# A graph-network block loop on one core: first relus put ahead of the gathered rows' work, next block's transposes put between the halves of the second layer

## The reference, cut to what matters

```python
h0 = layernorm(x)                                   # 6250 nodes x 256
out1 = segment_sum(edge_attr, dst)                  # 100000 edges x 96, dst is sorted
out2 = where(cnt > 0, segment_max(edge_attr, dst), 0)
out3 = out1 / max(cnt, 1)
h = concat([h0, out1, out2, out3, u[0]], axis=1)
h = relu(h @ W1 + b1) @ W2 + b2                     # hidden 1024, out 256
x = x + (h + h0)
x = x + ffn(layernorm(x))                           # router, top 2 of 16 experts, layer norm
```

## Time and profile before

| | us |
|---|---|
| median of 3 runs | 1315.99 (1310.38 to 1318.45) |
| the profiled execution's own time | 1307.6 |
| its span in the profile | 1305.9 |
| TensorE busy in the span | 1129.7 (87%) |
| ScalarE busy | 647.9 (50%) |
| GpSimd busy | 830.1 (64%) |
| VectorE busy | 788.1 (60%) |
| mean granted TensorE clock | 0.925 of full speed |

### The profile page before, as it was taken

How to read it: one execution, slowest core, us unless ns; L and a number is a source line. 1 busy time by engine, 2 the same in 40 slices (tenths; PEclk the granted TensorE clock), 3 DMA queues, 4 the chain that set the end, 5 groups by cost and what they waited for, 6 DMA issues and landing times.

```text
span 1305.9 us, 27758 instructions
## 1 busy us (share of the span) xinstructions
PE 1129.7 (87%) x6584; PEld 973.4 (75%) x6585; DVE 788.1 (60%) x3031; ACT 647.9 (50%) x1972; POOL 830.1 (64%) x1112
## 2 busy tenths in 40 slices
PE   2007999999999999999999999999999999999354
PEld 1006888877888878888888888899999999998011
DVE  5989899799799989953444114642222222221697
ACT  5954566566656655665565342223332323333464
POOL 5767666775676566666665145656665666664786
PEclk7557999999999999999999999999999999999665
DMA  9976678768777677486111258756665666663665
GB/s 313 294 267 219 225 283 299 255 209 307 273 277 271 251 234 269 165 285 203 49 37 38 81 194 308 261 186 202 212 213 196 214 213 206 211 212 123 207 224 171
DMA packets 131052, 282.65 MB, mean 216 GB/s; under 512 B 25742, under 2 KB 38293, under 8 KB 130831
## 3 DMA queue, kind: packets, MB, share of 16 engines
q1 hardware_dynamic: 93947, 218.28, 49.4%
q0 software_dynamic: 26048, 43.47, 10.5%
q10 hardware_dynamic: 10964, 19.96, 4.4%
HBM read 167.15 MB, written 114.25 MB: 215 GB/s over the span
## 4 chain that ended last, share of the span: by engine, by line
PE 54%; DMA 11%; issue 11%; POOL 10%; ACT 7%; DVE 4%; POOLq 2%; ACTq 0%; SPq 0%; DVEq 0%
PE ps L1222 14%; PE ps L1230 14%; DMA mem<-piece_carry,mem 7%; PE ps L1112 6%; PE ps L1098 6%; PE ps L1100 6%; POOL mem L597 3%; POOL mem L596 3%; PE ps L1208 2%; DMA mem<-in_dst_dram,mem 2%; POOL mem L570 2%; ACT mem L883 2%; DVE ps L1625 1%; PE ps L1148 1%; PE ps L1102 1%
## 5 line engine op out<-in xcount | busy, mean ns | idle before, releaser
L987 ACT ACTIVATE mem<-ps,mem 128x128 f32<-128x128 f32 x452 | 129.3, 368 | 303.6 <-PE ps L1222 272.7
L1222 PEld LDWEIGHTS ps<-mem 128*128 128x128 f32 x1808 | 217.9, 192 | 9.4 <-issue 3.7
L1098 PE MATMUL ps<-mem 128*128 128x250 f32 x800 | 210.1, 386 | 17.0 <-ACT mem L883 15.6
L1222 PE MATMUL ps<-mem 128*128 128x128 f32 x1808 | 221.2, 276 | 1.8 <-issue 1.6
L1230 PE MATMUL ps<-mem 128*128 x904 | 214.6, 380 | 3.4 <-issue 3.3
L1317 DVE TENSOR_TENSOR_SCAN mem<-ps,mem 128x80 f32<-128x80 f32 x960 | 207.9, 301 | 0.3
L1321 DVE TENSOR_TENSOR_SCAN mem<-ps,mem 128x80 f32<-128x80 f32 x960 | 207.8, 302 | 0.0
L1100 PE MATMUL ps<-mem 128*128 128x250 f32 x800 | 205.9, 380 | 0.0
L697 POOL DMA_INDIRECT expert_rows<-mem x113 | 113.8, 1008 | 121.5 <-DVE mem L1581 59.9
L1112 PE MATMUL ps<-mem 128*125 128x256 f32 x800 | 181.0, 379 | 0.7 <-ACT mem L883 0.7
L1098 PEld LDWEIGHTS ps<-mem 128*128 128x128 f32 x800 | 153.9, 195 | 37.1 <-ACT mem L883 17.6
(11 more groups left out here) (257 smaller groups left out, 1683.6 us busy)
## 6 DMA issues: line engine op xcount, KB each, us to landing
mem<-in_L_ffn_w_dram SPq DMA_DIRECT2D x129, 512.0 KB
run_sum<-mem SPq DMA_DIRECT2D x80, 480.0 KB
run_max<-mem SPq DMA_DIRECT2D x80, 480.0 KB
mem<-in_edge_attr_dram SPq DMA_DIRECT2D x72, 480.0 KB
mem<-expert_rows SPq DMA_DIRECT2D x22, 512.0 KB, 5.4
x_rows<-mem ACTq DMA_DIRECT2D x25, 256.0 KB, 4.7
x_normed<-mem ACTq DMA_DIRECT2D x25, 256.0 KB
mem<-in_x_dram ACTq DMA_DIRECT2D x24, 256.0 KB, 4.4
```

The costliest lines, as they stand in the source:

```text
L987: ins = act.activation(hT[b][:, c, :], bank(2 + b, c * P, (c + 1) * P), ACT.Relu, bias=eb1c[:, bass.ds(e, 1), c])
L1098: pe.matmul(h, W1x[:, c, hc * P:(hc + 1) * P], XT[b][:, c, :], start=(c == 0), stop=False)
L1222: ins = pe.matmul(bank(2 + b, f * P, (f + 1) * P), w1now[q][:, c, f * P:(f + 1) * P], XgT[b][:, c, :], start=(c == 0), stop=(c == DC - 1))
```

## The change

On ScalarE `carry_in` moves from ahead of `relu(i, 0)` to behind `take_logits`. `take_turned` moves behind `write_x2` and `store_x2`, and `take_g` ahead of `take_x2`. On TensorE `turn(i+1)` moves from ahead of layer 2 to between its halves, and `turn_x2(i-1)` from between the halves to behind them. No instruction is added or removed, and GpSimd, VectorE and SyncE keep their order.

```diff
@@ ScalarE, gnn_step
                 if more:
                     moments1(*after(i, g, b), 0)
                     moments1(*after(i, g, b), 1)
-                    carry_in(*after(i, g, b))
                 relu(i, 0)
                 if logit:
                     take_logits(i - 2)
+                if more:
+                    carry_in(*after(i, g, b))
                 if norm:
                     moments2(i - 1, 0)
                     moments2(i - 1, 1)
...
                 relu(i, 1)
-                if more:
-                    take_turned(*after(i, g, b))
                 if norm:
                     write_x2(i - 1)
                     store_x2(i - 1, to)
+                if more:
+                    take_turned(*after(i, g, b))
+                take_g(i, g, b)
+                if norm:
                     take_x2(i - 1)
-                take_g(i, g, b)
@@ TensorE, layer2
-            def layer2(i, g, b, between=None):
+            def layer2(i, g, b, between=None, behind=None):
...
                 ins.then_inc(g_psum, 1)
+                behind()
@@ TensorE, gnn_step
                 def between2():
+                    if not isinstance(i, int) or i + 1 < MACROS:
+                        turn(*after(i, g, b))
+                    if amid2:
+                        amid2()
+
+                def behind2():
                     if not isinstance(i, int) or i >= 1:
                         turn_x2(i - 1)
-                    if amid2:
-                        amid2()
                 layer1(i, g, b, between1)
                 if behind1:
                     behind1()
-                if not isinstance(i, int) or i + 1 < MACROS:
-                    turn(*after(i, g, b))
-                layer2(i, g, b, between2)
+                layer2(i, g, b, between2, behind2)
```

## The result

The changed kernel took 1323.5 us, the median of 20 runs (1319.8 to 1329.1), beside 1313.2 us for the kernel before (20 runs, 1300.4 to 1324.7). The medians differ by 10.3 us. The ratio is 1.0101, 95% interval 1.0077 to 1.0126, which is 13 us: a loss of about 1%. The ratios in this text leave out runs more than 1.5% above the fastest of their kernel (four of the 20 before, none of the change, and later one run of e3 at 4161 us and one of r2 at 1801 us), so they differ a little from the quotient of the medians, which are over all runs. The forecast was 1325 us and a ratio of 1.007, the likeliest case. The profiled execution has a span of 1322.7 us against 1305.9, of which 1.4 us arise ahead of the block loop, 13.3 in it and 2.1 behind it.

The account below looks back on a forecast made before the run. TensorE, 95% busy in the block loop, was taken as the bound. New waits of 28 + 1.6 + 2 + 1.5 + 1.1 = 34.2 us against 23 removed gave 11 us slower, 9 on the median: 1325 us, range 1307 to 1343.

Parts of the forecast that it names:

- The exchange of waits: TensorE, block loop: line 1098's relu wait under 3 us, new layer 2 relu wait some 22 times, 20 to 30 us.
- The chain of ScalarE: Relus, logits, `carry_in`, `moments2`, `mask_rows` per block: 16.94 us long, so second relus come 0.63 us after they could.
- The 0.8 us of `turn`'s place: Ahead of layer 2 on TensorE: without `turn` there, the first relu is no longer hidden, 0.8 us each block.
- The end of the loop: Block 24: router matmuls wait for `turn_x2`, `take_g` and `take_x2` behind layer 2; once, 1.1 us, between 0 and 1.5.
- The gathers (C): Rival: gathered rows too late even for `carry_in`'s new place, 10 to 20 us more, 1340 us; chance 0.13.
- what slips through: Late gathered rows or `moments1` in the block loop, mainly beside extra indirect DMAs: 1.5 us in all, between 0 and 10.
- the gain from the low clock: TensorE behind line 1098's waits: five low-clock stretches vanish, 1.4 to 1.5 us each, 7.3 us gained.
- The sign that was to speak for C: In the changed profile, ScalarE's wait for `piece_carry`, the gathered rows, over 10 us.
- The clock (B): Rival: TensorE's clock falls behind half of some 20 new layer 2 waits, 14 us more, 1339 us; chance 0.17.
- A, the relus not late: Rival: ScalarE's chain fits into 16.2 us, second relus aren't late, 3 to 8 us faster, 1308 to 1313; chance 0.17.
- part 1: `carry_in` behind the first relus on ScalarE: removes line 1098's 15.6 us of waits and five low clocks, 23 us gained.
- part 2: `turn` between layer 2's halves on TensorE: 1.4 us waits ahead of layer 2 in 20 blocks, 28 us, plus 1.6 us.

Follow-up runs that it names:

- e3: The whole change plus `norm_rows`, the two normalising activations ending `mask_rows`, moved behind the second relus; 1305.2 us, ratio 0.9945 to the kernel before.
- r2: e3 run again on the same chip as r1; 1304.5 us, ratio 0.9930 to the kernel before.
- e1: Kernel before with only `carry_in` moved behind the first relus and the logits on ScalarE; 1309.0 us, ratio 0.9991.
- e2: The change without the `carry_in` move: only the moves of `turn`, `turn_x2`, `take_turned` and `take_g`; 1320.4 us, ratio 1.0069 to the kernel before.
- b3: b1 with GpSimd's wait for the last indices in block 19 moved from ahead of `add_rows` to ahead of `gather`; 1287.9 us, ratio 0.9838 to the kernel before.
- b0: b1 with the two normalising activations left at the end of `mask_rows`; 1303.0 us, ratio 0.9955 to the kernel before.
- b2: b1 plus the change's moves of `turn`, `turn_x2`, `take_turned` and `take_g`; 1302.2 us, ratio 0.9950 to the kernel before.
- r1: The whole change again, unaltered, on a third chip; 1321.3 us, ratio 1.0056 to the kernel before.
- b1: Kernel before with `carry_in` behind the first relus, `moments1` and `moments2` earlier, normalising activations ahead of the wait for `join`; 1293.4 us, ratio 0.9858.

## Why the prediction was right, point by point

**The exchange of waits.** Forecast: line 1098's wait nearly gone (under 3 us), a new one of layer 2 some 22 times and 20 to 30 us. Measured 1.4 us, and 23 times 31.4 us, a little above that range. e1 and e2 show the two parts apart: `carry_in`'s new place takes the first away, `turn`'s new place uncovers the relu.

**The chain of ScalarE.** Forecast: second relus 16.86 us into a block, layer 2 at 17.38, blocks 25.9 us. Measured in block 4: 16.71, 17.22, 25.73, so 1.3 us more than b3's 24.41 without waits where I had 1.4. The sum from two blocks of the trace before was 0.15 us too long. The lateness of 0.63 us (16.71 - 16.23 = 0.48 measured in such blocks, 0.9 in blocks 12 to 17) is real and can be bought back by order alone, as e3 shows. `join` was hidden behind `moments2`, as forecast, but only just: b0, without `moments2` in between, has its second relus at 16.56 us, 0.15 earlier. Two chains of nearly the same length run side by side here, and to shorten one alone wins little.

**The 0.8 us of `turn`'s place.** Block 24 before the change showed it in advance, and b2 measured it at 0.79 for a block, with nothing else in the way.

**The end of the loop.** Forecast 1.1 us. The router matmuls of block 24 start at 775.65, 8.40 us behind layer 2's start (767.25), where before it was 761.07 - 753.63 = 7.44. That is 0.96 us more:

```profile
767.25 7.17 PE L1114 MATMUL ps<-mem 128*125 128x256 f32 x32 [0.73 <-ACT mem L883]
774.26 0.59 PE L1127 MATMUL ps<-mem 125*128 125x125 f32 x4
775.65 1.04 PE L1134 MATMUL ps<-mem 128*125 128x16 f32 x8 [0.80 <-ACT mem L922]
```

**The gathers (C).** The cover of half a microsecond held in every block but 14. I had counted 1.5 us for what slips through; block 14 alone was 4.3 us longer than its neighbours in the first profile (30.4 against 26.1), wait and low clock together, and 2.0 us in the second. This term was too small, and the gain from the low clock was too large by the 2.9 us of that stretch: 4.4 us instead of 7.3. The sign that was to speak for C was, by its letter, there:

```profile
ACT mem L831 <- DMA mem<-piece_carry,mem: 11.5, 2, 10.3
```

That is over 10 us, but 10.3 of it end at 96.29, ahead of the loop, and in the loop only the 1.2 us of block 14 remain (in r1 1.7 of 6.8). The sign should have left out what lies ahead of the loop, as 5.3 of the 25.0 us in the earlier trace rows do.

**The clock (B).** In the first profile it fell once in the loop, behind the wait of 3.06 us in block 14; in r1 not there, behind 3.60 us, but behind the 2.24 us of block 19, which had left it up in the first. It never fell behind the 21 other waits of layer 2, 0.7 to 1.6 us each, in either. The windows of r1:

```profile
620.90:624.30 3.40, 3.40 (x9) 2.65 (x9) 3.30 (x4) 1.77 (x5) 1.53 (x1) 0.51 0.21 80
486.00:496.00 10.00, 6.40 (x38) 5.64 (x35) 10.00 (x48) 6.59 (x17) 5.84 (x7) 1.00 0.60 205
```

The Trainium skill's rule in "TensorE: Matmul & The Clock Gate", section "A second HAM failure mode: psum-queue depth-cycling", that frequent short idle times make the clock swing, is not what these waits did: there was one in each block, and the clock stood at 1.00 from 300 to 400 us. The section has it of another kernel and gives no length or spacing of such idle times. By that rule I had 1339 us; the measurement decides for 1323.5.

**A, the relus not late,** fell with the start of the relus at 16.7.

**The sum.** 11 us against the profiled execution, of which I put 9 on the median, since the profiled one lay under it; the comparison of 20 runs gave 13 us by the ratio (10 by the medians) and the repeat 7 (6). The discount had no ground in a row, and the plain sum was the better estimate of the first. That 1325 came within 1.5 us of 1323.5 is in part luck: the base of three runs, 1316.0, was 2.8 us above the median of 20, and the loss was put too low by 1 to 4 us. Within the sum, too, errors cancel: 0.15 us too much in the ordinary blocks, too little for blocks 12 to 17, 19 and 14.

**A step that only the experiments found wrong:** that gains and losses of the two parts add. In e2 the added 0.8 us for a block took away part of the waits that part 1 removes, so part 2 alone cost 9 to 11.5 us and not 19. For the whole change, where those waits are gone anyway, the sum held.

## What to carry to other kernels

When an engine's work is moved behind something that another engine waits for, add up everything that then stands between two such points: here relus, `carry_in`, `moments2` and `mask_rows` had 8.5 us from the first to the second relus and needed 9.0, while ScalarE idled ahead of the first relus. Add up the ways through other engines as well: b0 took the 2.3 us of `moments2` out of this stretch and won 0.15, because `join` on GpSimd ended no earlier. And a piece of TensorE work of its own, such as the transposes, is worth most just where TensorE would otherwise wait for the first result of another engine; moved elsewhere it costs that latency in every round. Once both are right the next stop may be a wait placed too early in an engine's list, as the last indices' in b1.

## What the runs showed of the hardware that was not expected

The length of an idle time did not decide about the clock by itself. In the kernel before, the clock was low from 602.7 us on, behind a wait of line 1098 of 0.93 us that followed the router's narrow matmuls; in the changed kernel the waits of up to 1.63 us between wide matmuls left it at 2.4 GHz in both profiles, and the longer ones (2.24 and 3.06 us in one profile, 2.24 and 3.60 in the other) had the low clock behind them once each time, at different ones. So a long wait makes it possible, not certain. Two runs show it side by side, both in block 19, with the same matmuls ahead of the wait and behind it. In b0 the clock fell, in e1 it did not (each time the matmul behind the wait, and a stretch of busy time with the granted clock as the third number from the end):

```profile
605.08 0.43 PE L1079 MATMUL ps<-mem 125*128 125x125 f32 x2 [1.87 <-ACT mem L869]
606.00:609.40 3.40, 3.40 (x11) 2.77 (x10) 3.30 (x4) 2.76 (x7) 1.60 (x2) 0.50 1.10 348
```

```profile
609.30 0.43 PE L1080 MATMUL ps<-mem 125*128 125x125 f32 x2 [1.88 <-ACT mem L869]
609.30:616.00 6.70, 6.70 (x38) 6.00 (x39) 5.07 (x7) 4.21 (x10) 3.78 (x4) 1.00 0.40 123
```

The block was 28.0 us long in b0 and 26.4 in e1. What decided between the two is not shown. Whether the narrow matmuls ahead are what made 0.93 us enough was not tried.

The spread of the runs shrank with the waits for gathered rows: 1300 to 1325 us before (20 runs), 1320 to 1329 with the change (20 runs), 1287 to 1292 us in b3 (six runs). That the one causes the other was not tested.
